# Node attention of a decoder kernel: the fold of the angles moved to another step, and the mask products issued for two query tiles in turn

## The reference, cut to what matters

```
member = one_hot(tk_idx, 4).sum(-2) > 0           # top 2 of 4 router logits
pos = cumsum(member) - member                     # place of a token in a node
for n in range(4):
    qr = q * cos[pos_n] + rotate_half(q) * sin[pos_n]   # kr likewise
    scores = where(causal & member_n, qr @ kr.T * 64**-0.5, -1e9)
    outs[n] = softmax(scores) @ v
y = tk_w[0] * outs[first choice] + tk_w[1] * outs[second choice]
```

## Time and profile before

| | |
|---|---|
| median of 3 runs | 1853.75 us (1850.45 to 1855.61) |
| the profiled execution | 1856.05 us, span 1854.3 us |
| granted TensorE clock, mean | 0.855 of full speed |
| busy over the span | PE 1372.8, PEld 1037.9, DVE 1114.4, ACT 714.3, POOL 384.8 us |
| fold L996 | 16 times, mean 1057 ns |
| mask products L908 | 256, 45.0 us busy |
| `find_top` L1088 | 128, 65.1 us busy |

### The profile page before, as it was taken

How to read it: one execution, slowest core, us unless ns; L and a number is a source line. 1 busy time by engine, 2 the same in 40 slices (tenths; PEclk the granted TensorE clock), 3 DMA queues, 4 the chain that set the end, 5 groups by cost and what they waited for, 6 DMA issues and landing times. The chain is left out here.

```text
span 1854.3 us, 24940 instructions
## 1 busy us (share of the span) xinstructions
PE 1372.8 (74%) x8853; PEld 1037.9 (56%) x8853; DVE 1114.4 (60%) x2412; ACT 714.3 (39%) x1537; POOL 384.8 (21%) x400
## 2 busy tenths in 40 slices
PE   4898898888866897674674975758735977868785
PEld 3676666666745565561453964545623764744662
DVE  5899998999545576324556536443436648435634
ACT  4456666656313464232231221004102425645451
POOL 2565566665210100110101310000001000000000
PEclk8899899998878799796786986759967997989897
DMA  6011011010010100340002510000020002000100
GB/s 219 22 42 38 25 42 36 27 42 15 1 59 1 35 1 1 122 137 0 1 13 76 173 52 1 1 1 1 1 91 0 1 1 44 2 1 5 40 2 12
DMA packets 31611, 63.97 MB, mean 35 GB/s; under 512 B 6785, under 2 KB 18177, under 8 KB 30977
## 3 DMA queue, kind: packets, MB, share of 16 engines
q1 hardware_dynamic: 30464, 60.15, 10.5%
q0 software_dynamic: 1024, 2.23, 0.5%
HBM read 54.13 MB, written 4.18 MB: 31 GB/s over the span
## 5 line engine op out<-in xcount | busy, mean ns | idle before, releaser
L188 POOL TENSOR_TENSOR rstd<-spread,minus_half 128x4 f32<-128x4 f32 x36 | 36.8, 1023 | 1001.9 <-DVE spread L170 1001.9
L918 PE MATMUL l0h_scores<-l0h_k_rot,l0h_q_slots 128*128 128x128 f32 (+1 forms) x1024 | 206.6, 349 | 0.0
L918 PEld LDWEIGHTS l0h_scores<-l0h_k_rot,l0h_q_slots 128*128 128x128 f32 x1024 | 169.9, 208 | 13.1
L1135 POOL TENSOR_TENSOR l0h_k_part<-large_weights,l0h_sines 128x512 f32<-128x512 f32 x64 | 83.9, 1311 | 177.2 <-PE l0h_scores L918 129.1
L1009 ACT ACTIVATE l0h_scores<-l0h_scores,l0h_top 128x128 f32<-128x128 f32 (+1 forms) x256 | 100.4, 392 | 27.9 <-DVE l0h_top L1088 27.7
L1082 DVE TENSOR_TENSOR l0h_q_slots<-l0h_q_rot,l0h_chosen 128x1024 f32<-128x1024 f32 x64 | 78.4, 1225 | 6.7
L894 PE MATMUL l0h_projected<-XT,l0h_wq 128*128 128x256 f32 x256 | 70.2, 398 | 15.3 <-ACT large_weights L980 12.0
L908 PE MATMUL l0h_scores<-l0h_key_masks,l0h_query_picks 4*128 4x128 bf16 (+1 forms) x256 | 45.0, 257 | 49.2 <-DVE l0h_probs L1105 49.1
L1136 POOL TENSOR_TENSOR l0h_k_rot<-large_weights,l0h_cosines 128x512 f32<-128x512 f32 x64 | 80.9, 1264 | 0.0
L1088 DVE TENSOR_REDUCE l0h_top<-l0h_scores 128x2 f32<-128x256 f32 (+1 forms) x128 | 65.1, 548 | 6.4 <-PE l0h_scores L918 6.4
L1447 ACT ACTIVATE l0n_probs<-l0n_scores,l0n_top 128x256 f32<-128x256 f32 x128 | 53.8, 483 | 39.0 <-DVE l0n_top L1478 38.9
(11 more groups left out here) (762 smaller groups left out, 3585.8 us busy)
## 6 DMA issues: line engine op xcount, KB each, us to landing
l1e_experts<-in_l_experts SPq DMA_DIRECT2D x16, 768.0 KB, 4.3
l0e_experts<-in_l_experts SPq DMA_DIRECT2D x15, 578.0 KB, 4.0
l0h_chosen<-l0h_chosen_dram SPq DMA_DIRECT2D x64, 128.0 KB, 2.9
small_weights<-in_w_l_ffn SPq DMA_DIRECT2D x1, 4016.0 KB, 12.1
l0h_pos<-l0h_pos_dram SPq DMA_DIRECT2D x56, 64.0 KB, 2.0
large_weights<-in_w_l_xattn SPq DMA_DIRECT2D x1, 2632.0 KB, 9.0
l3f_late<-l3f_values SPq DMA_DIRECT2D x2, 1040.0 KB, 7.0
l0h_wq<-in_l_wq SPq DMA_DIRECT2D x16, 128.0 KB, 2.9
```

What stands on the lines that cost most here:

```text
L918: mm = nc.tensor.matmul(at[:, slot], q_slots[:, s % 2, slot, part, i * P:(i + 1) * P], k_rot[:, s % 2, part, 0:KEYS[i][1]], start=False, s ...
L1135: nc.gpsimd.tensor_tensor(k_part[:], source, at_batch(sines, s), ALU.mult)
```

## The change

The fold of a head moves from the last step of the head two before it (behind `copy_turned`, ahead of the next step's exponents) to the first step of the head just before it, right ahead of that head's sines. The mask operands stand twice in SBUF, in rows 0 to 3 and in rows 64 to 67, so that tile 0 takes them from row 0 and tile 1 from row 64, and SP issues four transfers for them instead of two. All four mask products of a step are issued first, in the order slot 0 of tile 0, slot 0 of tile 1, slot 1 of tile 0, slot 1 of tile 1; the hiding products and the f32 products of both tiles follow. What is computed is the same.

```
-        key_masks = sb("key_masks", [NODES, 2, N], BF16)
-        query_picks = sb("query_picks", [NODES, 2, CHOICES, N], BF16)
+        key_masks = sb("key_masks", [P // 2 + NODES, 2, N], BF16)
+        query_picks = sb("query_picks", [P // 2 + NODES, 2, CHOICES, N], BF16)
+        rows_of_tile = lambda i: slice(i * P // 2, i * P // 2 + NODES)
...
+                    for i in range(TB):
+                        sp.dma_start(key_masks[rows_of_tile(i), h % 2], absent_dram[h * NODES:(h + 1) * NODES])\
+                            .then_inc(masks_loaded[h % 2], 16)
+                        sp.dma_start(query_picks[rows_of_tile(i), h % 2],
+                                     chosen_dram[:, h * NODES:(h + 1) * NODES].rearrange("o r s -> r o s"))\
+                            .then_inc(masks_loaded[h % 2], 16)
...
-                    pe.wait_ge(masks_loaded[h % 2], 32 * (h // 2 + 1))
+                    pe.wait_ge(masks_loaded[h % 2], 64 * (h // 2 + 1))
+                    for slot in range(CHOICES):
+                        for i in range(TB):
+                            query = slice((TB * b + i) * P, (TB * b + i + 1) * P)
+                            rows = rows_of_tile(i)
+                            nc.tensor.matmul(unit(scores, s, i)[:, slot], query_picks[rows, h % 2, slot, query],
+                                             key_masks[rows, h % 2, b * S:b * S + KEYS[i][1]], start=(slot == 0),
+                                             stop=False, skip_group_check=True)
                     for i in range(TB):
                         at = unit(scores, s, i)
-                        query = slice((TB * b + i) * P, (TB * b + i + 1) * P)
-                        for slot in range(CHOICES):
-                            nc.tensor.matmul(at[:, slot], query_picks[:, h % 2, slot, query],
-                                             key_masks[:, h % 2, b * S:b * S + KEYS[i][1]], start=(slot == 0), stop=False,
-                                             skip_group_check=True)
...
                     if b == 0 and 1 <= h < H0 - 1:
+                        fold(h + 1)
                         sines_of(h + 1)
                     if b == 2 and h + 2 < H0:
                         turns(h + 2)
-                    if b == 3 and h + 2 < H0:
-                        fold(h + 2)
```

## The result

| | before | changed |
|---|---|---|
| median of 22 runs each | 1852.88 us (1849.28 to 1858.58) | 1849.32 us (1842.04 to 1851.76) |
| ratio of the runs, 95% interval | | 0.9967 (0.9956 to 0.9979) |
| profiled execution | 1856.05, span 1854.3 | 1851.08, span 1849.4 |
| head stage, from `find_top` of step 1 to the last `combine` | 431.8 us | 428.4 us |
| the rest, behind the last `combine` of the head stage | 1362.1 us | 1361.1 us |

A forecast was written before the change was run, and what follows sets the result against it. DVE was taken to bound the head stage (403 of 444 us busy). Terms -0.35 - 1.05 - 1.1 + 0.6 = -1.9 us gave 1851.9 from 1853.75, rounded to 1852, forecast as no change; range 1847 to 1859.

The forecast's parts named there:

- (b): Third step of heads 5, 9 and 13: score at half clock, DVE waits 1.15 us for the query; -0.35 each, -1.05.
- (a): The start: `find_top` of step 0 waits for tile 1 at half clock; -0.35 us.
- The saving per score: Grouped masks on PE save 0.25 us per step (0.23 serial, 0.34 overlapped), 0.35 at half clock.
- The rival that alternation stalls PE: Changing between rows 0 and 64 drains PE's array, each score 0.07 to 0.1 us longer; 1859 us; chance 0.12.
- (c): Heads 1, 2, 6, 10, 12, 14, query only just late: about 0.2 us each goes entirely, -1.1.
- my clock rivals: PE's half clock in third steps: none falls (about 1847 us, chance 0.12) or all fall (about 1857, chance 0.08).
- (d): Groups of heads 3, 7, 11: PE's saving 3 x 0.25 against the fold's 0.96; +0.2 each, +0.6 us.
- The fold at no cost in ordinary heads: Second step's exponents come 0.34 us later; slack 0.40 in six heads, 0.67 in heads 1 and 9; no cost.
- The rival that ACT bounds the second step: Each head's second step: exponents shift 0.96 instead of 0.34 us, beyond 0.40 slack; +4.1, 1856 with other terms; chance 0.08.
- SP's transfers at no cost: Two more transfers per head, 0.30 us of issue each, fit in SP's wait; no cost, uncovered 0.6 per head.
- The saving only lengthens that idle time: Outside the listed places PE waits for `combine`, so its saving of 0.25 us only adds idle time.
- My own mark for being wrong: Wrong if DVE waited for exponents in most heads' second step, or shed more than 4 us of waits.

The follow-up runs named there:

- e6: Kernel before, with masks loaded twice and tile 1's taken from row 64, product order and fold as before: ratio 0.9999 (0.9987 to 1.0011).
- e3: Changed kernel with both tiles' masks in row 0 (two transfers instead of four), new product order kept: ratio 0.995 (0.9934 to 0.9966).
- e4: Changed kernel with POOL's key rotation of a third step held until DVE has reduced the next head's angles: ratio 0.9915, 1839.21 us.
- e2: Kernel before with only the fold moved as in the change, masks left as they were: ratio 1.0021, 1858.82 us.
- e8: The same kernel as e3, measured a second time: ratio 0.9976 (0.9964 to 0.9988).
- e1: Changed kernel with the fold left in its old place (masks alone): ratio 0.9934, 1842.76 us against 1856.77 before.
- e5: e1 with POOL's key rotation held as in e4: ratio 0.9908, 1836.15 us.
- e9: Kernel before, with ten unused products on PE before the third step's score in heads 1, 2, 5, 6, 9, 10, 13, 14: ratio 0.9942.
- e10: Changed kernel with the same ten unused products on PE as e9: ratio 0.9951, 1845.97 us.

## Why the prediction was right and wrong

I forecast no change, and there is one: the sum of terms was -1.9 us, and the measured ratio is three times that. That 1852.0 lies only 2.7 us from the measured median is in part luck, since some of the misses cancel. The mechanism (PE's saving counts only where a query is late) is what the traces show. The steps that failed are two. In term (b), "-0.35 each, -1.05", I priced three long waits at what a score becomes shorter; they went whole, -3.7 us, because the half clock behind them lasted 3.4 us and not 6.8. And DVE's reductions beside POOL were put at nothing; they changed by -2.3 us in the ordinary heads and by +2.85 in heads 3, 7 and 11. Term by term:

- **(a), the start.** Step 1 begins 0.5 us earlier (59.87 against 60.41), near the 0.35. But the same point lies at 59.0 in e6, which saves nothing in a score, so the start alone shows nothing.
- **The saving per score.** 0.25 taken, 0.32 measured. I took the serial end since the rows showed no two products at once. From first mask to hiding product e3 shows the serial case, 0.43 (0.42 worked out, a saving of 0.21), and the changed kernel 0.32. Here I had set the rule against the rows: the Trainium skill's TensorE: Matmul & The Clock Gate, Part 3, says that products in different row groups overlap. The trace agrees: 0.32 is about the 0.31 that I had worked out for two at once. The rival that alternation stalls PE is refuted.
- **(b) and (c), the third steps.** I sized them at the saving, 0.35 and 0.2, -2.15 together. The waits went entirely, -4.8 with all nine of them (three of 1.23, six of 0.13 to 0.25; the one in head 12 is in its fourth step, not its third). In (c) that is as forecast, as those waits were shorter than the saving. For (b) the step that failed is "-0.35 each": a wait of 1.15 to 1.23 vanished, since the long stretches of half clock became short ones. That is the first of my clock rivals (chance 0.12) by half: the clock still fell in nearly every head, but for some 3.4 us and not for 6.8. Why it did so in all three profiles of the changed kernel (and in e4), and in none of e2, e3, e6, e8 and the kernel before, is not settled; e1 and e5, with the same masks and the fold in its old place, still have one such wait of 1.10 and two of 1.2 and 1.4. What is shown is that the waits hang on the clock. The fourteen profiles have twenty stretches of 6.8 us ahead of the last head, all outside heads 3, 7 and 11, and each comes with a wait of 0.83 to 1.36; no other wait for a query in those heads is over 0.27. With PE busy (e9) the waits are gone from the ordinary heads of the old kernel too. The premise of that rival, that PE falls to half clock in some third steps "and not in others with like idle time", was misread: in the kernel before it fell in all eight heads with 2.9 us, and only the lengths differed.
- **(d), the chunk heads.** I forecast +0.2 for each group and +0.6 in all. Measured from step 12 to step 19 it is +1.36 in the first group (134.55 to 183.66 against 135.90 to 183.66), +0.36 in the second and +1.35 in the third, +3.1 in all. The reductions (next point) are 2.85 of that. The waits alone come to +0.2, near the forecast, but only because two missed sizes cancel. One is the fold: "DVE's delay is caught up by the wait for PE" is wrong. ACT has the fold behind the chunk's copy, and DVE waits 0.86 for the exponents of steps 13, 29 and 45:

```profile
138.47 1.05 ACT L1000 ACTIVATE l0h_cosines<-l0h_sines 128x1024 f32<-128x1024 f32 x1
...
145.99 0.19 DVE L1097 RECIPROCAL l0h_scores<-l0h_total 128x4 f32<-128x4 f32 x1 [0.86 <-ACT l0h_scores L1013]
```

  In heads 3 and 11 the query of the third step is late as well, by 0.71, where it was late by 0.30 before. That is the clock: the score ahead of it on PE stands in a half-clock stretch (141.6 to 145.0, and from 363.4), which the kernel before did not have there. In head 7 the clock stays at full and that wait is nil, and in e10 it is nil in all three heads, at full clock too. The window of head 3:

```profile
141.60:145.00 3.40, 3.40 (x13) 2.98 (x13) 3.19 (x6) 3.37 (x8) 0.00 (x0) 0.50 0.00 0
```

  Against e1 a group is 1.26 us longer in head 7 and 2.25 in heads 3 and 11, where I had 0.96 for the fold. The other is the masks: the 0.75 a group was far too small, as e1 shows the waits of the three groups down from 7.9 to 2.4, 1.8 a group. In steps 17, 33 and 49 the wait was therefore not 0.2 longer, as I had said, but shorter: 0.51 in the view of DVE against 1.11, and it would be none without the fold.
- **DVE and POOL.** The step "DVE's 4.33 us unchanged" held, but nothing in my text asked what POOL, which starts when PE's scores or chunks are ready, would collide with once these came earlier. DVE gains 0.15 in ten heads and 0.8 in one, because L1066 now starts behind POOL's second multiplication (216.79, which ended at 216.75; before, it ran from 217.30 to 218.55, and L1063 started at 218.28) and no longer beside it, and loses 0.95 in each of heads 3, 7 and 11.
- **The fold at no cost in ordinary heads.** Right, and close: the exponents of step 25's kind are ready 0.04 us before DVE asks, 0.32 in heads 1 and 9; I had said 0.06 and 0.33. The rival that ACT bounds the second step is refuted there; it came true in the chunk heads, which I had excluded from it.
- **SP's transfers at no cost.** Right, by e6.
- **"The saving only lengthens that idle time."** Wrong: PE's idle time ahead of a third step's masks is 2.91 before and after in the eight ordinary heads that have it, though in heads 4, 8 and 12 it grew from 0.80 to 2.36. PE ends its work before that gap with `project_q`, which must wait until DVE has read the previous one, so it moves with DVE and not with PE's own saving.
- **My own mark for being wrong**, DVE shedding more than 4 us of waits: 3.7 us in the view (20.2 to 16.5), 4.4 in my table, with 5.3 from the queries alone. The text was on the border, as the time was.
- **Slips in the sums.** With 0.34 and 0.45 the terms add up to -3.1, not -2.8. In the rival on ACT the shift beyond the slack is 0.56, not 0.59, which makes +3.9. The chances 0.60, 0.14 and 0.11 leave 0.15 unsaid.

Between the two profiled executions the stage comes to: ordinary heads -7.9 (waits for queries -4.8, reductions -2.3, the rest short waits), groups +3.1, the last two steps +1.4, where the last score is at half clock: -3.4 us. So the end of the stage, which my sum left at nothing, is a third size missed. The rest of the 5.0 us between the two executions is 1.0 behind the stage, where nothing was edited, and 0.5 ahead of it.

**What stays open.** Apart from the length of the clock's falls: e9's stage shortened by 1.8 us in its profile while its median fell by 9.5. Its profiled execution was its slowest, and the part behind the stage took between 1353.5 and 1363.3 us over the fourteen profiles, without an edit there. e10 is the reverse, a stage 4.3 us shorter and hardly a gain in the runs. So of the 6 to 8 us by the ratios the stage shows 3.4, and the rest has no place in a trace. How much of any version's gain comes from where half-clock stretches happen to fall in the later part wasn't tried.

## What to carry to other kernels

A mask product with few rows cost here about 0.1 us to enter and 0.1 to leave, as much as a pair's 0.107 or 0.213 in columns, so issue all of them together. Different row groups for two independent sets saved 0.11 us more in a score, too little to be told in the time of the whole kernel. Before costing an edit by its own instructions, look for the places where the critical engine waits by a clock or a shared port: there a few tenths decide over whole microseconds, in both directions. Work moved "into slack" must be checked at the exceptional steps (here three heads of sixteen), since they paid for nearly all of its cost.

## What the hardware showed that I had not expected

**DVE and POOL exclude each other.** In the fence of head 3 above, POOL's first multiplication ends at 163.55; L1068, which started at 162.46, ends at 164.63, which is 1.22 (its length when alone) behind 163.41; and POOL's second multiplication, recorded from 163.51, ends at 165.75, 1.12 behind that, against 1.27 alone. So each stood until the other was through, to within 0.15 us, rather than both running slower. The Trainium skill, SBUF — State Buffer, in the section on SBUF's two separate sides, says that VectorE and GpSimd share a pair of ports that one of them holds for a whole instruction; the trace agrees. Who comes first decides who stands: in the same place before, L1065 started 0.13 us ahead of POOL and kept its 1.22, and POOL took 2.23. In the kernel before, 14 pairs of reductions took 33.4 us; free of collisions they take 26.7.

**PE's two row groups overlap.** Four mask products on 4 rows each take 0.32 us with the change to the hiding product in turns of rows 0 and 64, and 0.43 all in row 0.

**Half clock behind short idle time.** 2.9 us without work for PE were followed by a granted clock of 0.50 (1.2 GHz instead of 2.4) in all eight such heads of the kernel before and of the changed one, but in only four of the eight in e1, so the idle time alone doesn't decide. At half clock tile 1's eight pieces of a score take 3.52 us instead of 1.89. Some 2.5 us of products nobody reads, put into that idle time, kept the clock at full speed in all eight scores, and the kernel before became 0.58% faster with them, against 0.33 to 0.44% by the change, with intervals that overlap.
